# Scores of heads i and i+8 as two 64-row tiles of the array, with their maxima split on GpSimd before they are turned

## The reference, cut to what matters

```python
x = x + 0.5 * ffn(layernorm(x))      # units 0 to 7, one for each sequence
x = x + dilated_attention(layernorm(x))   # "mid", one for each sequence
x = x + 0.5 * ffn(layernorm(x))      # units 8 to 15

def ffn(x):
    x = conv1d(x, width 3)                               # 128 -> 128 channels
    q, k, v = split(x @ wqkv.T + bqkv)                   # 16 heads of 8 channels
    scores = einsum('bhqd,bhkd->bhqk', q, k) / sqrt(8)   # 16 x 512 x 512 for each sequence
    attn = softmax(scores)
    x = layernorm(x + (attn @ v) @ wo.T + bo)
    probs = softmax(x @ gate_w + gate_b)                 # 8 experts, all are computed
    y = relu(x @ w1[e] + b1[e]) @ w2[e] + b2[e]          # 128 -> 512 -> 128, e = 0..7
    return layernorm(x + sum_e probs[e] * y[e])
```

## Time and profile before

| | before |
|---|---|
| median of 3 runs (lowest, highest) | 1839.16 us (1838.27, 1841.56) |
| the profiled execution: its time, its span | 1839.75 us, 1838.0 us |
| busy: PE, PEld | 1721.2 us (94%), 960.3 us (52%) |
| busy: DVE, ACT, POOL | 1391.6 us (76%), 1082.7 us (59%), 966.4 us (53%) |
| mean granted TensorE clock | 0.979 of full speed |
| DMA | 99.46 MB, 18.3% of 16 engines on the hardware queue |

### The profile page before, as it was taken

How to read it: one execution, slowest core, us unless ns; L and a number is a source line. 1 busy time by engine, 2 the same in 40 slices (tenths; PEclk the granted TensorE clock), 3 DMA queues, 4 the chain that set the end, 5 groups by cost and what they waited for, 6 DMA issues and landing times.

```text
span 1838.0 us, 29109 instructions
## 1 busy us (share of the span) xinstructions
PE 1721.2 (94%) x8605; PEld 960.3 (52%) x8752; DVE 1391.6 (76%) x2967; ACT 1082.7 (59%) x1964; POOL 966.4 (53%) x829
## 2 busy tenths in 40 slices
PE   3888999999999999999999999999999999999977
PEld 1224555555555555555555555555555555555555
DVE  4777777776777788778787887778778777767787
ACT  2465666666666656666565665656656566665633
POOL 5312556565655656556564655656555565655232
PEclk7799999999999999999999999999999999999988
DMA  4311112021221212122121211212122121210111
GB/s 124 84 48 56 49 32 76 25 73 36 68 49 33 76 38 76 47 59 62 37 75 39 81 47 33 82 33 80 44 61 63 36 68 31 76 36 31 36 37 27
DMA packets 89773, 99.46 MB, mean 54 GB/s; under 512 B 14928, under 2 KB 65920, under 8 KB 89600
## 3 DMA queue, kind: packets, MB, share of 16 engines
q1 hardware_dynamic: 88336, 93.40, 18.3%
q0 software_dynamic: 1280, 4.20, 0.8%
HBM read 77.63 MB, written 20.19 MB: 53 GB/s over the span
## 4 chain that ended last, share of the span: by engine, by line
PE 73%; DVE 18%; issue 4%; ACT 2%; DMA 2%; SPq 1%; POOL 0%; DVEq 0%; ACTq 0%; POOLq 0%
PE ctx_ps L1027 11%; DVE negmax L743 6%; PE score1b L1014 5%; PE score1a L1014 5%; PE hid_ps L899 5%; PE y_ps L899 5%; PE hid_ps L903 5%; PE y_ps L903 5%; PE y_ps L900 5%; PE hid_ps L900 5%; PE score2b L1007 4%; PE score2a L1007 4%; DVE x1n L703 3%; DVE hidh L714 3%; PE misc L899 1%
## 5 line engine op out<-in xcount | busy, mean ns | idle before, releaser
L496 POOL TENSOR_TENSOR hidl<-hid,hidh 128x512 fp32r<-128x512 f32 x456 | 589.8, 1293 | 593.1 <-DVE hidh L714 581.3
L619 ACT ACTIVATE hid<-hid_ps,cols 128x512 f32<-128x512 f32 x484 | 333.0, 688 | 380.3 <-PE hid_ps L903 365.3
L743 DVE TENSOR_REDUCE negmax<-score1a 128x1 f32<-128x512 f32 x512 | 350.7, 685 | 208.9 <-PE score1a L1014 206.3
L595 ACT ACTIVATE probs<-score2a 128x512 f32<-128x512 f32 x512 | 305.1, 596 | 140.2 <-PE score2a L1007 80.4
L743 DVE TENSOR_REDUCE negmax<-score1b 128x1 f32<-128x512 f32 x512 | 349.3, 682 | 32.5 <-PE score1b L1014 30.9
L595 ACT ACTIVATE probs<-score2b 128x512 f32<-128x512 f32 x512 | 303.5, 593 | 24.5 <-PE score2b L1007 24.4
L1027 PE MATMUL ctx_ps<-probs,V 128*9 128x512 f32 x2048 | 269.2, 598 | 1.2
L899 PE MATMUL hid_ps<-x1h,w1h 128*128 128x512 f32 x484 | 258.3, 534 | 2.7 <-ACT x1h L604 2.7
L714 DVE CAST hidh<-hid 128x512 fp32r<-128x512 f32 x512 | 244.0, 477 | 12.8 <-ACT hid L619 12.3
L1014 PE MATMUL score1a<-Kp,Qp 96*128 96x512 bf16 x512 | 199.1, 389 | 29.1 <-DVE negmax L743 12.0
L1014 PE MATMUL score1b<-Kp,Qp 96*128 96x512 bf16 x512 | 199.4, 390 | 21.2 <-DVE negmax L743 18.9
(11 more groups left out here) (181 smaller groups left out, 2229.8 us busy)
## 6 DMA issues: line engine op xcount, KB each, us to landing
gate_b<-gate_dram SPq DMA_DIRECT2D x128, 256.0 KB, 3.7
q_parts_dram<-q_parts SPq DMA_DIRECT2D x48, 128.0 KB, 2.3
k_parts_dram<-k_parts SPq DMA_DIRECT2D x48, 128.0 KB, 2.3
Qp<-q_parts_dram SPq DMA_DIRECT2D x64, 96.0 KB
Kp<-k_parts_dram SPq DMA_DIRECT2D x64, 96.0 KB
gate_b<-in_L_ffn_w POOLq DMA_DIRECT2D x16, 256.0 KB, 3.7
Qp<-q_parts_dram SPq DMA_DIRECT2D x64, 64.0 KB
Kp<-k_parts_dram SPq DMA_DIRECT2D x64, 64.0 KB
```

What stands on the lines that cost most here:

```text
L496: pool.tensor_tensor(hidl[:, n % RING, :], hid[:, n % 2, :], hidh[:, n % RING, :].bitcast(F32), ALU.subtract).then_inc(s["h_lo"], 1)
L595: act.activation(probs[:, n % 2, j, :], score2[(T - P2_AT) % 2][:], ACT.Exp, scale=SCALE)\
L619: act.activation(hid[:, n % 2, :], hid_bank(u, n)[:], ACT.Relu, bias=col(n))\
L743: dve.tensor_reduce(negmax[:, g % 2, T % 16:T % 16 + 1], score1[T % 2][:], AX.X, ALU.max, negate=True).then_inc(s["a_max"], 1)
```

## The change

Heads i and i+8 form a pair. Each pair's rows stand in one `Qp`/`Kp` column block: head i in partitions 0 to 50, head i+8 in partitions 64 to 114 (48 rows of products, 3 of the maximum). Both phases do a pair at a time, at even ticks only: two matmuls, one for each half of the partitions, into the two banks of one PSUM tensor, and then one DVE reduction or one ACT exponential over both banks (1024 elements). The next pair of matmuls waits until that one is done. The maxima are split in three on POOL, while they still stand as 128x16, and the 48 columns of parts are turned by one bf16 matmul against a bf16 identity; ACT copies the result out and SP sends two DMAs in place of three. `Qp` and `Kp` are double-buffered by the unit's parity, and loaded in two chunks (pairs 0 and 1, then pairs 2 to 7) of six DMAs for each of q and k. At the start POOL's two big memsets and DVE's small one are replaced by four POOL memsets of 32 partitions each.

```diff
-SCORE_ROWS = 96
-MAX_ROW = 96
+PAIRS = H // 2
+HALF = 64
+SCORE_ROWS = 48
+MAX_ROW = 48
+ALL_ROWS = MAX_ROW + 3
+LOAD_CHUNKS = ((0, 2), (2, PAIRS))
...
-        score1 = [psum("score1a"), psum("score1b")]
-        score2 = [psum("score2a"), psum("score2b")]
+        score1 = ctx.enter_context(nc.psum_tensor("score1", [128, 2, 512], F32))
+        score2 = ctx.enter_context(nc.psum_tensor("score2", [128, 2, 512], F32))
...
-        LOADS_AT = ({-19: 0, -6: 1, 9: 2, 25: 3}, {-16: 0, -6: 1, 9: 2, 25: 3})
+        LOADS_AT = {-19: (0, 0), -16: (1, 0), -7: (0, 1), -5: (1, 1)}
...
                 # SP
-                if T - 2 in NM_AT:
-                    g = NM_AT[T - 2]
-                    wait_sp(s["a_m3"], u.count(4, g + 1))
-                    wait_sp(s["pack_zero"], 2)
-                    for part in range(3):
-                        sp.dma_start(Qp[MAX_ROW + part:MAX_ROW + part + 1, g * HG:(g + 1) * HG, :],
-                                     m_parts[:, part, :]).then_inc(s["a_m_in"], 16)
+                if T - 1 in NM_AT:
+                    g = NM_AT[T - 1]
+                    wait_sp(s["a_mr"], u.count(4, g + 1))
+                    for half in range(2):
+                        at = HALF * half + MAX_ROW
+                        sp.dma_start(Qp[u.parity][at:at + 3, 2 * g:2 * g + 2, :], m_rows[24 * half:24 * half + 24, :])\
+                            .then_inc(s["a_m_in"], 16)
...
                 # POOL, set_up
-                pool.memset(Kp[:].bitcast(F32), 0.0).then_inc(s["k_zero"], 1)
-                pool.memset(Qp[:].bitcast(F32), 0.0).then_inc(s["pack_zero"], 1)
...
+                pool.wait_ge(s["f_rs"], 1)
+                for k in range(4):
+                    at = HALF * (k % 2) + HALF // 2
+                    pool.memset(Kp[k // 2][at:at + HALF // 2].bitcast(F32), TWO_ONES).then_inc(s["pack_ones"], 1)
...
                 # POOL, tick
+                if T + 2 in NM_AT:
+                    g = NM_AT[T + 2]
+                    top, mid_part, low = (nm_parts[:, :, part, :] for part in range(3))
+                    wait(pool, s["a_max"], u.count(32, 8 * g + 8))
+                    wait(pool, s["a_nmT"], u.count(4, g))
+                    pool.tensor_copy(top, negmax[:, g % 2, :, :]).then_inc(s["a_n1"], 1)
+                    wait(pool, s["a_n1"], u.count(4, g + 1))
+                    pool.tensor_tensor(nm_rest[:], negmax[:, g % 2, :, :], top, ALU.subtract).then_inc(s["a_nr"], 1)
+                    wait(pool, s["a_nr"], u.count(4, g + 1))
+                    pool.tensor_copy(mid_part, nm_rest[:]).then_inc(s["a_n2"], 1)
+                    wait(pool, s["a_n2"], u.count(4, g + 1))
+                    pool.tensor_tensor(low, nm_rest[:], mid_part, ALU.subtract).then_inc(s["a_n3"], 1)
...
                 # DVE
-                if 0 <= T < 64:
...
-                    wait(dve, s["a_s1"], u.count(64, T + 1))
...
-                    dve.tensor_reduce(negmax[:, g % 2, T % 16:T % 16 + 1], score1[T % 2][:], AX.X, ALU.max,
+                if 0 <= T < 64 and T % 2 == 0:
+                    k = T // 2
...
+                    wait(dve, s["a_s1"], u.count(32, k + 1))
...
+                    dve.tensor_reduce(negmax[:, g % 2, :, k % 8], score1[:], AX.X, ALU.max,
                                       negate=True).then_inc(s["a_max"], 1)
...
                 # PE, T in NM_AT
-                    wait(pe, s["a_max"], u.count(64, 16 * g + 16))
-                    pe.transpose(misc[0:HG * TC, 0:128], negmax[:, g % 2, :], ident[:]).then_inc(s["a_nmT"], 1)
+                    wait(pe, s["a_n3"], u.count(4, g + 1))
+                    pe.matmul(misc[0:3 * HG * TC, 0:128], nm_parts[:].rearrange("p t a k -> p (t a k)"), ident_b[:],
+                              start=True, stop=True).then_inc(s["a_nmT"], 1)
...
                 # PE, scores
-                    wait(pe, s["a_max"], u.count(64, T - 1))
-                    pe.matmul(score1[T % 2][:], Qp[0:SCORE_ROWS, h, qc * 128:(qc + 1) * 128],
-                              Kp[0:SCORE_ROWS, h, :], start=True, stop=True).then_inc(s["a_s1"], 1)
+                if 0 <= T < 64 and T % 2 == 0:
...
+                    wait(pe, s["a_max"], u.count(32, k))
+                    for half in range(2):
+                        rows = slice(HALF * half, HALF * half + SCORE_ROWS)
+                        last = pe.matmul(score1[:, half, :], Qp[p][rows, pair, qc * 128:(qc + 1) * 128],
+                                         Kp[p][rows, pair, :], start=True, stop=True)
+                    last.then_inc(s["a_s1"], 1)
```

More of the change, by code:

```diff
@@ L196, in chunks @@
             return tile[:].rearrange("p (c d) -> p c d", c=TC)
+        s["pack_in"] = [sem(f"pack_in{k}") for k in range(len(LOAD_CHUNKS))]
         s["parts_out"] = [sem("q_parts_out"), sem("k_parts_out")]
@@ L228, in wait_misc @@
                     u = i - ago - (MID_FIRST if b == "mid" else b)
-                    name = "a_r1" if n == "a_m3r" else n
-                    wait(pe, s[name], per * u + k)
+                    wait(pe, s[n], per * u + k)
                     return
@@ L269, in hid_bank @@
         def hid_bank(u, n):
-            return score1[0] if alone(u, n) and n % 2 else hid_ps
+            return score1[:, 0, :] if alone(u, n) and n % 2 else hid_ps[:]
         def wait_lo(eng, u, k):
@@ L338, in tick @@
                     if T == at:
[L339 removed]
+                        for chunk_in in s["pack_in"]:
+                            wait_sp(chunk_in, u.count(CHUNK_LOADS, 0))
                         for part, written in enumerate(("f_p1", "f_p2", "f_p3")):
@@ L343, in tick @@
                                 .then_inc(s["parts_out"][k], 16)
-                for k, (Tk, g) in [(k, at) for k in range(2) for at in LOADS_AT[k].items()]:
-                    if T != Tk:
-                        continue
+                if T in LOADS_AT:
+                    k, chunk = LOADS_AT[T]
+                    lo, hi = LOAD_CHUNKS[chunk]
                     wait_sp(s["parts_out"][k], u.count(48, 48))
-                    wait_sp(s["a_s2"], (u.n - 1) * 64 + 16 * g + 16)
-                    wait_sp(s["pack_zero"], 2)
-                    wait_sp(s["pack_in"], u.count(PACK_LOADS * G, PACK_LOADS * g + PACK_LOADS // 2 * k))
-                    hs = slice(g * HG, (g + 1) * HG)
-                    for row, n, part, step in RUNS_OF_PARTS[k]:
-                        src = dram[k][part:part + (n if step else 1), :, hs, :].rearrange("a d h q -> a d (h q)")
-                        if not step:
-                            src = src.to_broadcast([n, DH, HG * S])
-                        sp.dma_start((Qp, Kp)[k][row * DH:(row + n) * DH, hs, :].rearrange("p h q -> p (h q)"), src)\
-                            .then_inc(s["pack_in"], 16)
@@ new lines, in tick @@
+                    for half in range(2):
+                        for row, n, part, step in RUNS_OF_PARTS[k]:
+                            src = dram[k][part:part + (n if step else 1), :,
+                                          PAIRS * half + lo:PAIRS * half + hi, :]\
+                                .rearrange("a d i q -> a d (i q)")
+                            if not step:
+                                src = src.to_broadcast([n, DH, (hi - lo) * S])
+                            at = HALF * half + row * DH
+                            sp.dma_start((Qp, Kp)[k][u.parity][at:at + n * DH, lo:hi, :]
+                                         .rearrange("p i q -> p (i q)"), src).then_inc(s["pack_in"][chunk], 16)
@@ new lines, in tick @@
+                    wait(pe, s["a_exp"], u.count(32, k))
+                    for half in range(2):
+                        rows = slice(HALF * half, HALF * half + ALL_ROWS)
+                        last = pe.matmul(score2[:, half, :], Kp[p][rows, 2 * g + j, kc * 128:(kc + 1) * 128],
+                                         Qp[p][rows, 2 * g + j, :], start=True, stop=True)
+                    last.then_inc(s["a_s2"], 1)
+                if 0 <= T < 64 and T % 2 == 0:
+                    k = T // 2
+                    pair, qc = divmod(k, TC)
+                    for chunk_in, (first_pair, _) in zip(s["pack_in"], LOAD_CHUNKS):
+                        if qc == 0 and pair == first_pair:
+                            wait(pe, chunk_in, u.count(CHUNK_LOADS, CHUNK_LOADS))
+                    wait(pe, s["a_max"], u.count(32, k))
+                    for half in range(2):
+                        rows = slice(HALF * half, HALF * half + SCORE_ROWS)
+                        last = pe.matmul(score1[:, half, :], Qp[p][rows, pair, qc * 128:(qc + 1) * 128],
+                                         Kp[p][rows, pair, :], start=True, stop=True)
+                    last.then_inc(s["a_s1"], 1)
@@ L1019, in tick @@
                     g, kc = divmod(n, TC)
-                    wait(pe, s["a_exp"], u.count(64, 4 * n + 4))
+                    wait(pe, s["a_exp"], u.count(32, 2 * n + 2))
                     if n == 0:
@@ L1026, in tick @@
```

(5 more changed lines are left out.)

98 lines of the change are left out of this document (42 added, 56 removed).

## The result

The changed kernel takes 1925.18 us (median of 4 runs, 1916.77 to 1932.79), the kernel before 1839.45 us (4 runs, 1838.27 to 1841.56). The ratio is 1.0461, with a 95% interval of 1.0429 to 1.0492: 86 us slower. The forecast was 22 us slower and the range ended at 1905. The sign is right, the size is not. The profiled execution has a span of 1927.6 us where the one before had 1838.0.

A forecast was written before the change was run, and what follows sets the result against it. PE was taken as the bound, busy 102.7 of 105.0 us. Per steady iteration -6.9 + 7.4 + 1.0 = +1.5, times 14 = +21, and +1 at the start, gave 1861 us; range 1755 to 1905.

The forecast's parts named there:

- The pairs run together: Score matmuls on PE: 64 pairs replace 128 single ones per unit; overlapping halves save 14.1 us.
- The POOL chain: Turnings of the maxima: PE waits for POOL's four split operations, 7.4 us a unit, bounds 0 and 12.
- +1: Start and first iteration together: 3 us gained on normalisation and memsets, 4 lost on pairs bounded by reduction plus latency.
- The changes of tile: PE entering and leaving 64-row tiles and turnings: 3.2 + 3.2 + 0.8, 7.2 us an iteration in all.
- later reductions: Longer DVE reductions delay the gate and the experts' low part: 1.0 us a unit, range 0 to 4.
- so there is room; nothing: SP's DMA queue: the six-pair chunk, 1.2 MB at ticks 57 and 59, costs nothing at 0.2 share.
- every price was taken at a granted clock of 1.00: Steady-state PE prices came from the earlier trace at full granted clock; no term for a lower clock there.
- times 14: Steady state: the net of +1.5 us an iteration counted over 14 iterations, +21 us.
- (1): Rival: 64-row tiles cost nothing to enter or leave, 101 us more gained, 1760; chance 0.20.
- (2): Rival: PE does not wait for POOL at the turnings, 104 us less, 1757; chance 0.10.
- (3): Rival: the halves of a pair don't overlap on PE, 197 us more, 2058; chance 0.05.
- (4): Rival: with one buffer and later reductions PE waits 4 us an iteration, not 1.0: +42, 1903; chance 0.10.

The follow-up runs named there:

- both: Changed kernel with the turning of the maxima two ticks later and the packed rows loaded in three chunks: 1756.52 us, ratio 0.9557 to the kernel before.
- same_tile: The kernel with later turning and three chunks, but both halves of a pair use the same 64-row tile, one after the other: 1961.2 us.
- whole_array: The kernel with later turning and three chunks, but each half of a pair reads the same 65 rows, taking the whole array: 1885.64 us.
- three_chunks: Changed kernel with the second chunk cut in two, pairs 4 to 7 loaded at ticks 3 and 5 of the next iteration: 1898.65 us.
- late_turn: Changed kernel with the turning on PE and the copy and DMAs behind it two ticks later, POOL's split unmoved: 1822.4 us, ratio 0.9919.
- load_behind: Changed kernel with later turning, its whole 1.2 MB second chunk issued at ticks 1 and 3 of the next iteration: 1839.41 us, ratio 0.9997.
- load_slot: Changed kernel with later turning, its whole 1.2 MB second chunk issued at ticks 5 and 6 of the next iteration: 1788.77 us, ratio 0.9714.
- filled_wait: Changed kernel with three load chunks, plus 24 bf16 matmuls of 128 columns in front of the wait at each turning: 1873.88 us, ratio 1.0184.

## Why the prediction was wrong in size and right in sign

**Terms that held.** The pairs run together. The POOL chain makes PE wait: 7.4 us a unit were forecast, 98.8 us over 14 iterations are 7.1, and 7.2 us an iteration is what it costs (106.8 against 99.6). That sum has some luck in it. T = 17 was forecast at 1.1 us and T = 33 at 2.1, and both came out so, but T = 49 and T = 65 were forecast at 2.1 as well and measure 1.2 and 2.8.

The net of all else was forecast, with the wait left out, at -5.9 us an iteration; the kernel both shows 99.6 for 105.0 and 106.0 for 110.8, so -5.4 and -4.8. In the whole time both is 82 below before, and 22 - 104 = -82; that the two agree so closely is luck, since 14 iterations of -5.4 or -4.8 make -71, and the other 11 us come from outside of them, where +1 was forecast. Inside the net two terms were too large and cancelled. The running together is worth 12.1 and 10.7 and not 14.1: PE's idle time in the windows shown goes from 2.0 to 3.3 us and from 2.7 to 5.1, in part for maxima (13.3 us over twelve iterations of both, 2.7 in same_tile); what the rest is, no run tells. The changes of tile cost 4.6 and 4.3 and not 6.4, since fewer of them cost anything: 26 entries and not 32, 11 exits and not 16. From the kernel before to whole_array everything else is +2.1 and +1.5, for 1.0 of later reductions and 0.8 at the turnings.

**Step 1 that failed: "so there is room; nothing"**, said of the chunk on SP's queue. It went by the mean load of the queue (0.2 of its engines' share), and the cost was in the order: 1.2 MB issued 4.5 to 8.6 us ahead of `m_xn` moved its landing from 4.5 to 11.4 us. With 0.4 MB in that place instead it gives 26.5 us back (three_chunks), on top of late_turn 66. The Trainium skill ("DMA: Bandwidth & Descriptors", Queues, rings and completion order) says that each DMA engine consumes the descriptors of a queue in ring order; the traces agree: whatever stood behind the burst was late (`m_xn` 11.4 us in after; the maxima's rows, 50.6 us of waits, in load_behind), and what stood ahead of it was not (`m_xn` 4.4 us in load_behind and load_slot).

**Step 2 that failed: every price was taken at a granted clock of 1.00.** It went by the earlier trace rows, where it is 1.00, but the change itself makes PE idle for up to 2.8 us at a time at the turnings, and behind such idle time the clock is often at its lower level, for 3.4 or 6.8 us at a time: 44 us in twelve iterations of after. filled_wait gives 24.8 us back with the wait left in place. In the steady iterations of before, filled_wait and both no idle time of PE is over 1.3 us, and the clock is at 1.00.

**Step 3 that failed: "times 14".** The wait was priced for the 14 iterations of the earlier trace rows, but there are 16 units of four turnings. The iterations around them were given +1 in all, for other reasons. How much this is worth is shown in part. At the eight turnings outside of the 14 iterations PE idles 7.1 us in after. From filled_wait to both 117.4 us go, 13.4 more than the 104 forecast, but the 1536 added matmuls go in that step too. The second iteration, which was priced at nothing, takes 80.3 us before, 88.8 in after, 89.0 in three_chunks and in filled_wait, 83.5 in late_turn and 80.7 in both. So more than half of its 8.6 us go with the later turning, although PE idles only 1.5 us at its turnings; by what path they arise stays open.

**How far the pieces reach.** Over the twelve iterations before takes 1306.8 us, after 1364.9, three_chunks 1344.9, filled_wait 1328.2 and both 1246.7. The queue's 20.0 and the clock's 16.7 taken off, 21.4 us over before remain, and the forecast was 12 x 1.5 = 18. So in the steady state the two missing steps account for the miss, within 3 us. Outside of the twelve the profiled executions differ by 31.5 us, where the forecast had 4, and less is known there. In medians the pieces are 22 forecast, 26.5 for the queue, 24.8 for the clock and 13.4, together 86.7, with 85.7 measured. That this comes out is no further evidence: the last three are differences of successive runs, so the sum only says again that both lies 82 below before. The order in which they are taken off matters too, as late_turn shows, so the single figures are those of the order after, three_chunks, filled_wait, both.

**The rivals.** (1) is refuted by same_tile and whole_array: the changes of tile cost 4.3 to 4.6 us an iteration. (2) is refuted by the 98.8 us of waits at the turnings. (3) is refuted by the pairs that start 0.22 us apart, where same_tile has 0.44. (4), coupling that makes PE wait 4 us an iteration, has the size but not the cause: the waits for maxima are 0.9 us in an iteration of after without a mid and 2.3 to 6.8 in one with, and those shrink to 1.6 to 1.9 when `m_xn` is early (three_chunks), with the single buffers as they are. The range missed because neither the queue nor the clock had a case of its own; together they are 51 us, and the highest case kept in the range, 1903, held none of them.

## What to carry to other kernels

When a change makes fewer and larger DMAs of many small ones, list what stands behind them on the same queue up to the next large gap, and price each at the bytes ahead of it; the low mean share of the queue gave no sign of it here. When an added chain ends at an instruction of the engine that bounds the kernel, move that instruction by the length of the chain before judging the rest: here two ticks turned 1925 into 1822, and with the loads cut, 1756.5. Price an added wait like these on PE at its length and something for the clock behind it, and count it in every unit, not only in the steady window.

## What the runs showed of the hardware

- Two bf16 matmuls of 48 or 51 rows on the two 64-row tiles, into two banks, start together and hold PE for 0.22 us, as long as one. To enter behind an fp32r matmul costs 0.09 us, to leave into one 0.20, and to leave into the column-tiled product with V nothing; over an iteration with 32 entries all changes of tile cost 4.3 to 4.6 us (same_tile against whole_array).
- Idle time of 2.8 us on PE was followed by 3.7 us at a granted clock of 0.54, in some iterations and not in others; 24 small matmuls put in front of each such wait kept the clock at 1.00 in the steady state and made the kernel faster by 24.8 us.
- Four dependent POOL operations on 16 elements a row start 0.48, 0.28 and 0.28 us apart, and PE is released 1.4 us after the first starts (758.50 to 759.90).
- A DMA of 256 KB behind 1.2 MB on the same queue lands in 10.5 to 13.4 us (after), behind 0.4 MB in 3.6 to 4.5 (three_chunks), and ahead of the 1.2 MB in 4.0 to 4.5 (load_slot).
